# A tower of patch DFT, MLP, state scan and GRU: W1 in two loads, the DFT on even and odd parts, Newton halves as one product

## What is computed

```python
fr = jnp.fft.rfft(x.reshape(B, C, S, 200), axis=-1)
feats = jnp.concatenate([jnp.abs(fr), jnp.angle(fr)], axis=-1)
h = gelu(feats @ W1 + b1) @ W2 + b2
...
inv_term = jnp.linalg.inv(I - 0.5 * dt * A)
A_bar = (I + 0.5 * dt * A) @ inv_term
B_bar = dt * (inv_term @ B)
...
```

## Time and profile before

| | |
|---|---|
| median of 3 runs | 947.96 us (947.41 to 948.64) |
| profiled execution | 949.37 us, of which the span is 947.6 |
| busy, share of the span | PE 90%, PEld 73%, DVE 60%, ACT 38%, POOL 9% |
| mean granted TensorE clock | 0.591 of 2.4 GHz |
| chain that ended last | PE 82%, ACT 5%, DVE 5%, DMA 4% (W1) |
| HBM | 4.70 MB read, 1.31 MB written |

### The profile page before, as it was taken

How to read it: one execution, slowest core, us unless ns; L and a number is a source line. 1 busy time by engine, 2 the same in 40 slices (tenths; PEclk the granted TensorE clock), 3 DMA queues, 4 the chain that set the end, 5 groups by cost and what they waited for, 6 DMA issues and landing times.

```text
span 947.6 us, 40752 instructions
## 1 busy us (share of the span) xinstructions
PE 850.9 (90%) x17213; PEld 693.1 (73%) x17213; DVE 572.2 (60%) x3471; ACT 359.7 (38%) x1960; POOL 80.8 (9%) x194
## 2 busy tenths in 40 slices
PE   7399999999899999999999999989989989988975
PEld 4256565677778778878878878878878878877775
DVE  2314241533776776776776776777776776776654
ACT  3245362643333433433433433433333333333322
POOL 3102020221100000000000000000000000000000
PEclk7599896999555555555555555555555555555555
DMA  2400000000000000000000000000000000000000
GB/s 67 122 11 1 1 1 1 1 1 1 3 3 7 6 3 6 7 3 6 6 4 6 6 3 6 7 3 6 6 4 6 6 3 7 6 3 6 6 4 8
DMA packets 7321, 8.61 MB, mean 9 GB/s; under 512 B 1111, under 2 KB 6425, under 8 KB 7139
## 3 DMA queue, kind: packets, MB, share of 16 engines
q1 hardware_dynamic: 6833, 6.00, 2.4%
q0 software_dynamic: 256, 0.01, 0.0%
q10 hardware_dynamic: 50, 0.00, 0.0%
HBM read 4.70 MB, written 1.31 MB: 6 GB/s over the span
## 4 chain that ended last, share of the span: by engine, by line
PE 82%; ACT 5%; DVE 5%; DMA 4%; issue 3%; SPq 0%; POOL 0%; POOLq 0%; DVEq 0%
PE ps L1338 40%; PE ps L1344 11%; PE ps L1195 8%; PE ps L1252 7%; DMA W_sb<-in_L_tok_W 4%; PE ps L1267 3%; DVE h_hi L406 3%; PE ps L1117 3%; PE ps L1352 3%; ACT addend L761 2%; PE ps L1165 2%; PE ps L1177 1%; PE ps L1184 1%; PE ps L1285 1%; ACT tanh_r L751 1%
## 5 line engine op out<-in xcount | busy, mean ns | idle before, releaser
L1338 PE MATMUL ps<-h_hi,w_first 128*128 128x8 f16 x2560 | 268.2, 170 | 55.4 <-DVE h_hi L406 54.9
L1338 PEld LDWEIGHTS ps<-h_hi,w_first 128*128 128x128 f16 x2560 | 220.8, 104 | 109.8 <-DVE h_hi L406 109.8
L1338 PE MATMUL ps<-h_hi,w_rest 128*128 128x8 f16 x5120 | 276.6, 168 | 0.0
L1338 PEld LDWEIGHTS ps<-h_hi,w_rest 128*128 128x128 bf16 x5120 | 241.6, 105 | 0.1
L1344 PE MATMUL ps<-h_lo,w_first 128*128 128x8 f16 x2560 | 159.4, 168 | 0.1
L751 ACT ACTIVATE tanh_r<-ps 128x16 f32<-128x16 f32 x320 | 58.6, 183 | 260.8 <-PE ps L1344 260.8
L1338 PE MATMUL ps<-rh_hi,w_first 128*128 128x8 f16 x1280 | 137.0, 173 | 11.9 <-DVE rh_hi L1020 1.0
L1338 PE MATMUL ps<-rh_hi,w_rest 128*128 128x8 f16 x2560 | 139.0, 168 | 0.0
L1338 PEld LDWEIGHTS ps<-rh_hi,w_first 128*128 128x128 f16 x1280 | 110.0, 104 | 39.0 <-DVE rh_hi L1020 1.1
L406 DVE TENSOR_TENSOR_SCAN h_hi<-coef,addend 128x32 f16<-128x32 f32 x320 | 73.2, 229 | 84.1 <-ACT addend L761 84.1
L1338 PEld LDWEIGHTS ps<-rh_hi,w_rest 128*128 128x128 bf16 x2560 | 122.3, 105 | 0.0
(11 more groups left out here) (195 smaller groups left out, 1338.3 us busy)
## 6 DMA issues: line engine op xcount, KB each, us to landing
x_sb<-in_x SPq DMA_DIRECT2D x4, 500.0 KB
out<-res SPq DMA_DIRECT2D x20, 64.0 KB, 2.0
W_sb<-in_L_tok_W SPq DMA_DIRECT2D x1, 637.6 KB
W_sb<-in_L_tok_W SPq DMA_DIRECT2D x1, 384.0 KB
wnat<-in_L_ffn_Wwr SPq DMA_DIRECT2D x1, 256.0 KB, 4.6
wnat<-in_L_ffn_Wwz SPq DMA_DIRECT2D x1, 256.0 KB, 7.9
wnat<-in_L_ffn_Ww SPq DMA_DIRECT2D x1, 256.0 KB, 7.2
dft_sb<-in_dft SPq DMA_DIRECT2D x1, 157.8 KB
```

Source lines behind the costliest of these rows:

```text
L1338: mm(gate(c, j, g, m), w[:, m * 128:(m + 1) * 128], state[:, k * NB:(k + 1) * NB], start=False, stop=False, skip_group_check=True)
```

## The change

1. W1 is loaded by two DMAs, 96 rows and 5 rows of each half; its user waits for both.
2. The DFT works on sums and differences. Sample n and sample 200 - n of a patch are added into `even` (101 columns, with samples 0 and 100 as they are) and subtracted into `odd` (99 columns) by `even_odd`, on VectorE for groups 0 and 1, on GpSimd for groups 2 and 3. The transposes read these. `copy_patches` writes the columns to `evenT` and `oddT` in the order channel, patch, batch. `spectra` is then one product for the real part, from `evenT` with the cosines, and one for the imaginary part, from `oddT` with the sines. The table comes in by three DMAs (100, 1 and 99 rows).
3. A Newton half is one product. `step_w` holds 2 I above -M (transposed) in its first 32 columns and zeros in the rest, `Xn` holds I above X; `DY` holds D and Y side by side, and zeros. The odd half multiplies `DY` with its own first 64 columns, and two of the four blocks of the result are the new X and Y; ScalarE copies them by two instructions.

```diff
+W1_ROWS = 96
...
-        dft_sb = sb("dft_sb", [KP, 2, 2, NF])
+        cos_sb = sb("cos_sb", [KP + 1, NF])
+        sin_sb = sb("sin_sb", [KP - 1, NF])
+        even = sb("even", [128, NP, NS, KP + 1])
+        odd = sb("odd", [128, NP, NS, KP - 1])
...
-        patT = sb("patT", [KP, 2, PT])
+        evenT = sb("evenT", [KP + 1, PT])
+        oddT = sb("oddT", [KP - 1, PT])
...
-        negMT = sb("negMT", [128, N])
...
-        eye2 = sb("eye2", [128, N])
-        XY = sb("XY", [128, 2, N])
-        Dn = sb("Dn", [128, N])
+        step_w = sb("step_w", [128, 128])
+        Xn = sb("Xn", [128, N])
+        DY = sb("DY", [128, 128])
...
-            return bank(k + (4 if (g, h) == (0, 1) else 0), KP)
+            return bank(k + (4 if (g, h) == (0, 1) else 0), KP - 1 if k else KP + 1)
...
+        parts_done = sem("parts_done")
...
-            return bank(b, N, N), bank(b, N, 2 * N)
+            return bank(b, 128, N), bank(b, 128, 2 * N)
...
+        def patch_columns(tile, h):
+            s0, s1, _ = patches(h)
+            return tile.rearrange("p (c s b) -> p s b c", s=NS, b=NB)[:, s0:s1]
+
+        def psum_columns(tile, h):
+            s0, s1, cols = patches(h)
+            return tile[:, 0:cols.stop - cols.start].rearrange("p (s b c) -> p s b c", b=NB, c=CP)
+
+        def even_odd(eng, ops, g):
+            xs = x_sb[:, g, :].rearrange("p (s n) -> p s n", s=NS)
+            eng.wait_ge(x_in[g], 16)
+            ops.tensor_copy(even[:, g, :, 0:KP + 1:KP], xs[:, :, 0:KP + 1:KP])
+            ops.tensor_tensor(even[:, g, :, 1:KP], xs[:, :, 1:KP], xs[:, :, 2 * KP - 1:KP:-1], ALU.add)
+            return ops.tensor_tensor(odd[:, g], xs[:, :, 1:KP], xs[:, :, 2 * KP - 1:KP:-1],
+                                     ALU.subtract).then_inc(parts_done, 1)
+
...
-            sp.dma_start(dft_sb[:], dft).then_inc(dft_in, 16)
+            sp.dma_start(cos_sb[0:KP], dft[:, 0, 0, :]).then_inc(dft_in, 16)
+            sp.dma_start(cos_sb[KP:KP + 1], dft[0:1, 1, 0, :]).then_inc(dft_in, 16)
+            sp.dma_start(sin_sb[:], dft[1:KP, 0, 1, :]).then_inc(dft_in, 16)
...
-            sp.dma_start(W1_sb[:], W1.rearrange("(k p) h -> p k h", p=NF)).then_inc(w1_in, 16)
+            for p0, p1 in ((0, W1_ROWS), (W1_ROWS, NF)):
+                sp.dma_start(W1_sb[p0:p1], W1.rearrange("(k p) h -> p k h", p=NF)[p0:p1]).then_inc(w1_in, 16)
...
-            for z in (XY[:].rearrange("p a n -> p (a n)"), Dn[:], negMT[:], AbarT[:].rearrange("p c n -> p (c n)"), states[:]):
+            for z in (Xn[:], DY[:], step_w[:], AbarT[:].rearrange("p c n -> p (c n)"), states[:]):
...
-            pool.tensor_scalar(eye2[:], ident[:, 0:N], 2.0, None, ALU.mult).then_inc(bf_ident, 1)
+            pool.wait_ge(consts, 16)
+            pool.tensor_copy(Xn[0:N, :], ident[0:N, 0:N]).then_inc(bf_ident, 1)
+            pool.tensor_scalar(step_w[0:N, 0:N], ident[0:N, 0:N], 2.0, None, ALU.mult).then_inc(bf_ident, 1)
...
+            pool.wait_ge(parts_done, 2)
+            even_odd(pool, pool, 2)
...
+                if n == 2:
+                    pool.wait_ge(parts_done, 3)
+                    even_odd(pool, pool, 3)
...
-                cols = patches(h)[2]
...
-                a.activation(patT[:, 0, cols], ps_patT(0, g, h)[:, 0:cols.stop - cols.start],
+                a.activation(patch_columns(evenT[:], h), psum_columns(ps_patT(0, g, h), h),
...
-                    a.activation(Dn[0:N, :], ps_nt, ACT.Copy).then_inc(dn_done, 1)
+                    a.activation(DY[0:N, 0:N], ps_nt[0:N, :], ACT.Copy).then_inc(dn_done, 1)
...
-                    a.activation(XY[0:N].rearrange("p a n -> p (a n)"), ps_nx, ACT.Copy).then_inc(xy_done, 1)
+                    a.activation(Xn[N:2 * N, :], ps_nx[N:2 * N, 0:N], ACT.Copy).then_inc(xy_done, 1)
+                    a.activation(DY[0:N, N:2 * N], ps_nx[0:N, N:2 * N], ACT.Copy).then_inc(xy_done, 1)
...
-                cols = patches(h)[2]
...
-                v.tensor_scalar(patT[:, 1, cols], ps_patT(1, g, h)[:, 0:cols.stop - cols.start], 0.0, None,
+                v.tensor_scalar(patch_columns(oddT[:], h), psum_columns(ps_patT(1, g, h), h), 0.0, None,
...
+            even_odd(dve, v, 0)
...
-            v.tensor_scalar(negMT[0:N, :], Mt[:, 0, :], -1.0, None, ALU.mult).then_inc(su_dve, 1)
+            v.tensor_scalar(step_w[N:2 * N, 0:N], Mt[:, 0, :], -1.0, None, ALU.mult).then_inc(su_dve, 1)
...
-            v.tensor_scalar(XY[0:N].rearrange("p a n -> p (a n)"), Mt[:].rearrange("p a n -> p (a n)"),
-                            scale0[:, 0:1], None, ALU.mult).then_inc(su_dve, 1)
+            v.tensor_scalar(Xn[N:2 * N, :], Mt[:, 0, :], scale0[:, 0:1], None, ALU.mult)
+            v.tensor_scalar(DY[0:N, N:2 * N], Mt[:, 1, :], scale0[:, 0:1], None, ALU.mult).then_inc(su_dve, 1)
...
+            even_odd(dve, v, 1)
...
-            dve.wait_ge(w1_in, 16)
+            dve.wait_ge(w1_in, 32)
...
-                dve.wait_ge(xy_done, NEWTON)
-                dve.wait_ge(bf_ident, 4 + NCOPY)
+                dve.wait_ge(xy_done, 2 * NEWTON)
+                dve.wait_ge(bf_ident, 5 + NCOPY)
...
-                    v.scalar_tensor_tensor(out=AbarT[0:N, i, :], in0=XY[0:N, 1, :], scalar=2.0 * S_SCALE,
+                    v.scalar_tensor_tensor(out=AbarT[0:N, i, :], in0=DY[0:N, N:2 * N], scalar=2.0 * S_SCALE,
...
-                    pe.wait_ge(x_in[g], 16)
+                    pe.wait_ge(parts_done, g + 1)
...
-                for k in range(2):
+                for k, part in enumerate((even, odd)):
...
-                        n0 = sg * PATCH + k * KP
...
-                                  x_sb[:, g, n0:n0 + KP], ident[:])
+                                  part[:, g, sg, :], ident[:])
...
-                        pe.wait_ge(dft_in, 16)
+                        pe.wait_ge(dft_in, 48)
...
-                for part, dst in ((0, ps_re(g, h)), (1, ps_im(g, h))):
-                    for k in range(2):
-
-                        v = patT[:, k, :].rearrange("p (s b c) -> p c s b", s=NS, b=NB)
-                        last = mm(dst, dft_sb[:, k, part, :], v[:, h * (CP // 2):(h + 1) * (CP // 2)],
-                                  start=k == 0, stop=k == 1)
+                for dst, table, part in ((ps_re(g, h), cos_sb, evenT), (ps_im(g, h), sin_sb, oddT)):
+                    last = mm(dst, table[:], part[:, h * HT:(h + 1) * HT], start=True, stop=True)
...
-                pe.wait_ge(xy_done if i % 2 else dn_done, i // 2 + 1)
+                if i % 2:
+                    pe.wait_ge(xy_done, i + 1)
+                else:
+                    pe.wait_ge(dn_done, i // 2 + 1)
...
-                    mm(ps_nt, eye2[:], eye[:], start=True, stop=False)
-                    mm(ps_nt, negMT[:], XY[:, 0, :], start=False, stop=True).then_inc(nt_psum, 1)
+                    mm(ps_nt, step_w[:], Xn[:], start=True, stop=True).then_inc(nt_psum, 1)
...
-                    mm(ps_nx[:, 0:N], XY[:, 1, :], Dn[:], start=True, stop=True)
-                    mm(ps_nx[:, N:2 * N], Dn[:], XY[:, 1, :], start=True, stop=True).then_inc(nx_psum, 1)
+                    mm(ps_nx, DY[:], DY[:, 0:2 * N], start=True, stop=True).then_inc(nx_psum, 1)
...
+            pe.wait_ge(bf_ident, 4)
...
-                        pe.wait_ge(xy_done, NEWTON)
-                        mm(bank(0)[:, 0:N], B_sb[:], XY[0:N, 1, :], start=True, stop=True).then_inc(b_psum, 1)
+                        pe.wait_ge(xy_done, 2 * NEWTON)
+                        mm(bank(0)[:, 0:N], B_sb[:], DY[0:N, N:2 * N], start=True, stop=True).then_inc(b_psum, 1)
```

## The result

The changed kernel takes 919.36 us (four runs, 915.03 to 922.14) where the kernel before, run beside it, took 947.68: ratio 0.971, interval 0.965 to 0.977, 28.3 us faster. Measured again beside other kernels it was 913.71 against 944.45, ratio 0.969 (0.965 to 0.973). The forecast was 903.0 with a range of 892 to 916: the sign was right, the size was not. The second median lies within the range, but 10.7 above the forecast.

The account below looks back on a forecast made before the run. Bound by W1's transfer to 42.7 us, then TensorE products to 230.2, then an untouched recurrent stage. 9.0 + 19.2 + 14.9 + 8.0 - 1.5 - 4.6 = 45.0 off the profiled 949.37 gave 904.4, median 903.0; range 892 to 916.

Parts of the forecast that it names:

- W1, the start, 9.0: Start of the token stage: W1 no longer late, first `up` at 33.5 instead of 42.5, 9.0 us gained.
- I set the start of the early Newton halves as before: Start: the shorter DFT's gain is taken back by ScalarE's passes and the wait behind group 1's even and odd parts.
- 0.15 us a half: Start: added cost of each of nine early Newton halves, from second copies and a wider product; 1.4 us in all.
- an engine with nothing else to do at that time: GpSimd, even and odd parts of groups 2 and 3: some 2.9 us a group, each due tens of us later.
- The DFT, 19.2: Token stage: six spectra halves on TensorE fall from 4.40 to 1.2 us each, 19.2 us gained.
- hides it: Token stage: spare time of several us between transposes and spectra hides the scattered patch copies, 0.5 us more if doubled.
- Newton, 14.9 less 4.6 for ScalarE: Token stage: 71 Newton halves each save 0.21 us on TensorE, 14.9 us; waits for ScalarE give back 4.6.
- ScalarE term: Token stage: faster TensorE waits around ScalarE's table loads and second Newton copies; 4.6 us given back.
- rival 2: Newton becomes a chain through ScalarE; if most halves wait, 10 of 14.9 us go: 913 us, chance 0.12.
- Rival 3: Newton halves: loads of full weights add up instead of hiding, the Newton term is 0: 918 us, chance 0.04.
- The clock, 8.0 less 1.5: Token stage: two half-clock drops vanish, 8.0 us gained; 1.5 given back at the stage's half-clock start.
- With the strided halves gone I expect both drops to go: Token stage: both clock drops, each beginning on a long strided DFT half, disappear; 8.0 us gained.

Follow-up runs that it names:

- w1_alone: The kernel before with only the two loads of W1; 939.52 us, ratio 0.992 to the kernel before.
- newton_alone: The kernel before with only the Newton halves as one product, W1 in one load and the old DFT; 938.79 us, ratio 0.994.
- eo2_late: The changed kernel with GpSimd's even and odd parts of group 2 waiting for the first angle; 917.25 us in one run.
- start_order: The changed kernel with its start reordered, no work added or left out, and GpSimd's group 2 parts behind the angle; 904.88 us, ratio 0.958.
- strided: The changed kernel with patch copies to adjacent columns again and the two DFT products reading columns 16 elements apart; 919.59 us, ratio 0.970.
- dft_alone: The kernel before with only the DFT on even and odd parts, W1 in one load and old Newton halves; 931.41 us, ratio 0.982.
- release: The changed kernel with even Newton halves waiting only for ScalarE's copy of X, the two kinds in different PSUM banks; 915.01 us, ratio 0.968.
- spread: The changed kernel with ScalarE's passes over the spectra in even pieces set singly between Newton copies, not three in a row; 915.41 us, ratio 0.967.

## Why the prediction was wrong

**W1, the start, 9.0: got 3.0.** The load spread as said; w1_alone moved the first `up` by 8.1. The step that failed is "I set the start of the early Newton halves as before" together with "0.15 us a half".
- Newton 0 started at 24.88 instead of 21.42, 3.5 later. Of this 2.0 is the queue: TensorE stood idle for 3.42 behind the odd part of group 1 and began its transposes at 21.51, before at 19.52. The shorter DFT did not pay for that. It began 2.7 later (12.56, before 9.82), behind `even_odd(0)` and the scattered copies, so that the second power, ahead of `even_odd(1)` on VectorE, ended only 1.3 sooner (20.20, before 21.49). The other 1.5 is the clock: the transposes and the bias row ran at half clock (the row 1.64, before 0.91). The edit is not shown to cause this, since w1_alone and newton_alone, which have no `even_odd`, show 1.64 too.
- The nine halves took 9.7 (24.88 to 34.62), before 7.2 (21.42 to 28.65): 2.5, forecast 1.4. A pair takes 2.09 instead of 1.43 (the earlier trace rows ends such a chain), at half clock in both kernels. The second copy is 0.2 of it; 0.5 is in the two products, from whose start to the copy 0.67 and 0.73 pass instead of 0.46. A likely reason, not tested, is that nothing runs there under which the full weight loads could hide.
- From the last copy to the angle's end 4.75 (34.62 to 39.37), forecast 3.35: the patch copy took 0.89 instead of 0.47 and held the arctangent back by 0.3, and GpSimd held the angle back by 1.2 (eo2_late). The prediction called GpSimd "an engine with nothing else to do at that time" and did not ask what its work does to VectorE's.

3.5, 1.1 and 1.4 are the 6.0 us that are missing. start_order brought the first `up` 6.4 sooner with the same instructions and the same half clock (its bias row took 1.64), so another order of the queues alone could make up for all of it. The prediction listed what queues behind `even_odd(1)` and then set the balance to nothing without adding it up.

On splitting at all the row was right: the rule of the Trainium skill that I weighed ("DMA: Bandwidth & Descriptors", section "Rules for kernel authors", on two transfers to disjoint partition ranges) would have left the first `up` at 42.5, and it came at 34.4. The same section of the Trainium skill asks for an outermost size that is a multiple of 16; 96 rows agree with that (in w1_alone W1's scaling starts at 30.82 and waits for no transfer), where 101 do not (34.65 us).

**The DFT, 19.2: right for the products.** 6.4 a piece in n = 2 and 4, which makes 19.3 if n = 0 gave as much, and strided shows both parts of the mechanism. The step that failed is that spare time "hides it" for the scattered copies: strided, without them, has n = 1 and 3 0.4 shorter and the first `up` 1.2 sooner.

**Newton, 14.9 less 4.6 for ScalarE: got 5.8.** Both terms were mis-sized. From one `up` to the next with three halves between is 2.77 (83.52 to 86.29) where dft_alone has 3.28:

```profile
97.55 0.91 PE L1275 MATMUL ps<-magT,W_sb 101*128 101x384 f32 x2
...
100.83 0.91 PE L1275 MATMUL ps<-magT,W_sb 101*128 101x384 f32 x2
```

That is 0.17 a half, not 0.21, or 12.1 for 71. Of it n = 2 and 4 kept 1.3 each (dft_alone against the changed kernel), n = 1 and 3 0.8 and 0.9, n = 5 0.2; for n = 0, which ran at another clock in the two, I take 1.3 as well. So about 6 went to waits, where 4.6 was forecast. The timeline shows some 0.9 a piece of them: in n = 2 0.34, 0.29 and 0.26 over the usual behind the products at 90.96, 94.06 and 97.54; in n = 1 1.13 at the arctangent, where the kernel before waited 0.51 already (its line below; the 0.16 of the earlier trace rows stands at the square root), and 0.25 behind a patch copy. The rest is not traced. This is the prediction's own ScalarE term, the passes and table loads, and rival 2 only in part: most halves do not wait, and the release took only 0.2 of the 0.9 out of an even piece, spread 0.4. Rival 3 did not come: in the token stage a half with full loads costs less than the old one.

```profile
84.38 0.71 PE L1267 MATMUL ps<-W_sb,hid 128*128 128x128 f32 x4 [0.51 <-ACT hid L702]
```

**The clock, 8.0 less 1.5: right in the profiled execution, the cause open.** Pieces n = 2 and 4 of before lost 2.9 and 5.6 against 29.6, and the changed kernel lost neither. "With the strided halves gone I expect both drops to go" agrees with the eleven profiles that lack them, but newton_alone kept them and lost nothing either, so chance is not ruled out. The drops come in some executions and not in others; the runs of before reach from 939.5 to 956.7. How much of this loss lies in the medians is not shown: the profiled execution of before, with two drops, lies 1.7 above the 947.68, that of newton_alone, with none, 4.3 below its own median. And the changed kernel has a half-clock stretch of uncertain length of its own, at n = 0.

**The sum.** 3.0, 19.3, 5.8 and 8.5 (the drops), less 0.4 in n = 1 and 3 (dft_alone against w1_alone), 0.4 at n = 0 (7.3 instead of 7.7) and 1.4 that the recurrent stage took more, make 34.4; 34.3 was measured. At the medians 6.0 of them are not there: the profiled execution of the changed kernel lies 4.3 below its median, that of before 1.7 above the one it is compared with. That leaves 28.3.

## What to carry to other kernels

Work that an edit adds ahead of a queue is priced by what stands behind it on every engine, not by the time it takes: with the instructions unchanged, their order at the start was worth 7.6 us in the profiled executions and 9 to 14 at the medians. When one late transfer goes, rebuild the whole chain that ends next, at the clock and beside the neighbours that it will have, before pricing the gain. And a clock drop seen in one execution is to be priced only after more executions, with the edit and without it, have shown how often it comes.

## What the runs showed of the hardware

- A GpSimd instruction with two operands in SBUF stops a VectorE instruction that reads SBUF until it is done: the angle ended at 39.37, 0.35 after GpSimd's instruction (37.54 to 39.02), and `bsum`, 0.15 us in w1_alone, took 1.14 beside one. It need not have two operands: `gbias`, a product with a constant, took 1.16 behind `bsum` in eo2_late instead of 0.17. The copy out of PSUM was not stopped (`oddT` at 39.29, 0.64, as long as ScalarE's of that size). The Trainium skill, "SBUF — State Buffer", section "SBUF: two separate sides", says that the two engines share a port pair under an exclusive lock; the trace agrees.
- Copies from PSUM that scatter single elements 160 B apart take 0.89 us for 384 columns instead of 0.47 (ScalarE) and 0.56 (VectorE).
- The clock column can miss a half-clock stretch: in the changed kernel's profile it reads 1.00 from 6 us on, while `up` products took 1.62 us at 39.51 and 0.89 at 44.92, as the earlier trace rows do at the two clocks. The duration of a known product is the safer reading.
- The recurrent stage, untouched, took 716.1 to 719.9 us over fourteen profiled executions.
